# A graph transformer's opening: the second root ahead of the key chain, and two weights' low halves traded between VectorE and GpSimd

## The chip, the cores and the metric

The kernel runs on one core of a Trainium2 chip. The metric is the device time of one execution in microseconds. The engines are TensorE (PE, with its weight loads PEld), VectorE (DVE), ScalarE (ACT), GpSimd (POOL) and SyncE (SP); each has its own instruction queue, executed in order, and they wait for each other through semaphores.

## The reference

Two layers on 1,250 nodes of 512 features, with 21,250 edges. The change lies in the first layer's first step:

```python
xn = _layernorm(x)
x = x + gnn(xn, edge_index, edge_weight, W, b) + mix(xn, w_qkv, w_out, b_out)
# gnn: deg = segment_sum(weights, dst) + 1; norm = dinv[src] * w * dinv[dst]
#      out = segment_sum((xn @ W)[src] * norm, dst) + b
# mix: q, k, v = split(xn @ w_qkv); q = elu(q) + 1; k = elu(k) + 1
#      kv = k^T v per head; out = (q kv) / (q . sum k); out @ w_out + b_out
```

So every normalised node tile is multiplied by four 512x512 weights: key (K), value (V), query (Q) and graph weight (H).

## The kernel before

**Tiles and halves.** The nodes are ten tiles of 128 rows (T = 10). Products keep fp32 accuracy with fp32r operands in two halves: the high half is a rounded copy (`_hi`, ScalarE), the low half is what is left (`_lo`, a subtraction), and a product of a tile with a weight is 4 blocks (one for each 128 of the 512 features) of 3 matmuls (high x high, high x low, low x high). For weight `i` the halves lie in `wsl[:, i, 0]` and `wsl[:, i, 1]`, each in four column blocks `c` of 128x512. For the tiles, TensorE transposes the normalised tile `xn` into the PSUM bank `pT`; `xt_hi(t)` on ScalarE and `xt_lo(t)` on VectorE write the halves of `xT`.

**Normalisation.** For each group of tiles the variance is followed by a root: a power of -0.5 in `root` on GpSimd (line 1015) or a square root on ScalarE, then four Newton steps on VectorE (lines 1311 to 1314) and `nmr` (line 1338), all on 128x5 tiles or smaller. The second root on GpSimd, `root(3, 5, T)`, is for tiles 5 to 9, whose first normalisation comes after pair 5.

**The order of the opening on TensorE**, written out by hand: transposes(0), K0, transposes(1), V0, K1, the edge rows, V1, transposes(2), kv(0), the base row, K2, kv(1), transposes(3), V2, then for t from 3 to 9 K(t), transposes(t+1), V(t), Q(t-3), H(t-3), kv(t). In the first of these rounds `kv(2)` stands behind K3, then a one-column product of `outside` (the count of edges outside their window), then a wait for the flag that VectorE makes of it. A product of tile t waits for `xt_lo(t)`; `kv(t)` = K(t)^T V(t) waits for `k_lo(t)` and `v_lo(t)`, which VectorE makes from the PSUM banks.

**The adjacency matrix.** The sorted edges lie in 170 columns of 128, taken as 85 pairs. Each pair is a product of one-hot matrices: the source one-hots (VectorE, `onehots(g)`, line 1438), times the edge weight's halves (GpSimd, `Loh`, line 1062), against the target one-hots `Roh` within a window (ScalarE for one column, lines 582 and 584, VectorE for the other, line 1440). TensorE places a pair's four matmuls (`adj(g)`, line 2111) between the blocks of the products from the 30th block on: pair 0 after the second block of V3, and the eighth pair, number 7, after the second block of H0. VectorE adds the result into `AT` (line 1469). The target one-hots need `key`, which GpSimd makes in a chain of five operations (lines 1049 to 1053) once VectorE has written `edge` (line 1431). There are four slots for the one-hots of pairs, so VectorE makes those of pairs 0 to 3 ahead.

**Who makes the low halves of the weights.** K and V: VectorE, block by block, in the opening. Q: `split_lo(WQ)` on GpSimd behind the key chain and the second root (line 1007). H: `wh_lo(c)` on VectorE (line 1389), two ahead of `k_elu(2)` and two behind `xt_lo(3)`.

Of the kernel before, what the change touches and what calls it, by code (L numbers as in the profile page):

```python
# [31 lines left out]
T = -(-N // P)  # L32
# [71 lines left out]
def build(nc, a, out):  # L104
    ctx = ExitStack()
    with ctx:
# [240 lines left out]
        for name, first_name, count in (  # L347
# [14 lines left out]
                ("ld_v1", "ld_w3", 16), ("ld_wp", "ld_wo", 16), ("ld_v2", "ld_x", 16), ("ld_xs", "out_st", 0), ("ld_wkb", "ld_small", 0), ("wv_hi", "wk_hi", KC), ("wh_lo", "wv_lo", KC), ("three_var", "c_pool", 1), ("ln_pow0", "pad_zero", 2), ("table_set", "oh_y", 0), ("ld_b2", "b_ld", 32),  # L362
# [137 lines left out]
        def _(act):  # L500
# [96 lines left out]
            split_k(0)  # L597
            ln_sqrt(2, 1, 2)
            split_k(1)
            xt_hi(0)  # L600
# [384 lines left out]
        def _(pool):  # L985
# [18 lines left out]
            def split_lo(i):  # L1004
                pool.wait_ge(S["w_hi"], i - 1)
                for c in range(KC):
                    ins = pool.tensor_tensor(wsl[:, i, 1, c], wraw[:, i, 1, c], wsl[:, i, 0, c].bitcast(F32), ALU.subtract)
                ins.then_inc(S["w_lo"], 1)
# [38 lines left out]
            st(pool.tensor_tensor(whl[:, :, 1], wf, whl[:, :, 0].bitcast(F32), ALU.subtract))  # L1047
            pool.wait_ge(S["edges_ok"], 5)
# [5 lines left out]
            root(3, 5, T)  # L1054
            split_lo(WQ)

            pool.wait_ge(S["keys_ok"], 1)
            for g in range(CP):
                pool.wait_ge(S["oh_src"], g + 1)
                w = whl[:, 2 * g:2 * g + 2, :].bitcast(F32).rearrange("p c (k n) -> p c k n", n=1).broadcast_to([P, 2, 2, P])  # L1060
                o = onehot_[:, g % SLOTS].rearrange("p c (k n) -> p c k n", k=1).broadcast_to([P, 2, 2, P])
                pool.tensor_tensor(Loh[:, g % SLOTS], o, w, ALU.mult).then_inc(S["oh_pool"], 1)  # L1062

# [236 lines left out]
        def _(v):  # L1300
# [86 lines left out]
            def wh_lo(c):  # L1387
                v.wait_ge(S["w_hi"], WH - 1)
                v.tensor_tensor(wsl[:, WH, 1, c], wraw[:, WH, 1, c], wsl[:, WH, 0, c].bitcast(F32), ALU.subtract).then_inc(S["wh_lo"], 1)
# [38 lines left out]
            xt_lo(2)  # L1428
            v2 = lambda x: x.rearrange("p (j c) -> p j c", c=2)
# [4 lines left out]
            ln_roots(3, 5, T, small[:, 2, 5:T])  # L1434
# [8 lines left out]
            def count_outside():  # L1443

                step(v.tensor_scalar(vd, vd, -1.0, 1.0, ALU.mult, ALU.add))
                step(v.tensor_tensor(rest[:, 2, :], wf, vd, ALU.mult))
                step(v.tensor_scalar(vd, rest[:, 2, :], 0.0, None, ALU.not_equal))
                v.tensor_reduce(outside[:], vd, AX, ALU.add).then_inc(S["rest_ok"], 1)
                v.wait_ge(S["rest_ps"], 1)
                v.tensor_copy(flagint[:], pA[0:1, 0:1]).then_inc(S["flag_ok"], 1)  # L1450
# [23 lines left out]
            wh_lo(0)  # L1474
            wh_lo(1)
            k_elu(2)
            xt_lo(3)
            wh_lo(2)
            wh_lo(3)
            k_lo(2)  # L1480
            v_lo(2)
            v.wait_ge(S["keys_ok"], 1)
            count_outside()
            v.wait_ge(S["flag_ok"], 1)
            v.load(count_reg, flagint[0:1, 0:1])
            for g in range(RSLOTS):
                onehots(g)
# [592 lines left out]
        def _(pe):  # L2080
# [34 lines left out]
            def product(t, w, done, bank=None):  # L2115
# [5 lines left out]
                for c in range(KC):  # L2121
                    if t == 0 and w < 2:
                        pe.wait_ge(S[("wk_lo", "wv_lo")[w]], c + 1)
                    if t == 0 and w == WQ:
                        pe.wait_ge(S["w_lo"], 1)
                    if t == 0 and w == WH:
                        pe.wait_ge(S["wh_lo"], c + 1 + after["wh_lo"])
# [608 lines left out]
```

## Time and profile before

| | us |
|---|---|
| Median of three runs | 583.02 (582.8 to 583.6) |
| The profiled execution | 583.02 |
| Its span | 581.3 |
| TensorE busy | 551.8 (95%) |
| VectorE busy | 452.1 (78%) |
| ScalarE busy | 321.4 (55%) |
| GpSimd busy | 278.6 (48%) |

The span runs from the first to the last instruction that the profile shows; 1.7 us of the time lie around it. Busy times of the engines overlap. A row of the timeline gives the start, the busy time, the engine, the line, the operation with output and input, and in brackets how long the engine had been idle and what released it.

### The profile page before, as it was taken

To read this page: it belongs to the slowest core of one execution; us is meant where nothing else is said; L and a number is where in the kernel's file an instruction comes from. 1 tells how busy PE (TensorE), PEld (TensorE's weight loads), DVE (VectorE), ACT (ScalarE), POOL (GpSimd) and SP (SyncE) were. 2 spreads that over 40 slices of the span, in tenths; PEclk is the share of its full clock that TensorE was granted. 3 is DMA by queue.
4 is the path that set the end of the run, shared out by engine and by line. 5 is a ranking of instruction groups with operands and counts; after the bars stand their busy time and mean duration, and the time that the engine had idled before them with its cause. 6 is when DMAs were issued, how large, how long until landed. Compare 5 with 4: busy or idle time off the path is not lost.

```text
span 581.3 us, 8775 instructions
## 1 busy us (share of the span) xinstructions
PE 551.8 (95%) x2947; PEld 451.8 (78%) x2947; DVE 452.1 (78%) x1048; ACT 321.4 (55%) x616; POOL 278.6 (48%) x326
## 2 busy tenths in 40 slices
PE   6968999999999999999999999999999999999997
PEld 4756888888888677888877766778877788778886
DVE  7977899989989688757858878768756765668986
ACT  7856889877855642213134765646455886432252
POOL 4455777777769126434833791002303673031553
PEclk9999999999999999999999999999999999999999
DMA  9500000000002011004104020000002000020004
GB/s 311 173 1 1 1 2 2 2 1 1 2 2 74 24 50 36 23 33 85 33 1 154 2 72 1 0 1 2 0 2 90 1 1 2 2 91 0 1 2 176
DMA packets 15078, 21.12 MB, mean 36 GB/s; under 512 B 3292, under 2 KB 6032, under 8 KB 15034
## 3 DMA queue, kind: packets, MB, share of 16 engines
q1 hardware_dynamic: 13674, 17.94, 9.7%
q10 hardware_dynamic: 1360, 2.62, 1.3%
q8 instruction: 24, 0.39, 0.3%
q14 instruction: 20, 0.16, 0.1%
HBM read 18.00 MB, written 2.56 MB: 35 GB/s over the span
## 4 chain that ended last, share of the span: by engine, by line
PE 60%; DVE 17%; POOL 8%; ACT 6%; issue 5%; DMA 2%; SPq 1%; DVEq 0%; ACTq 0%; POOLq 0%
PE p L2282 7%; PE p L2111 5%; PE pQ L2403 4%; PE p L2403 4%; PE pQ L2129 4%; PE p L2129 4%; PE pH L2129 4%; POOL qx L1236 2%; DVE p L1543 2%; PE p L2369 2%; PE pH L2294 2%; PE pKV L2369 2%; PE pKV L2158 2%; POOL xT L1224 2%; PE pH L2602 1%
## 5 line engine op out<-in xcount | busy, mean ns | idle before, releaser
L1062 POOL TENSOR_TENSOR Loh<-onehot,whl 128x512 fp32r<-128x512 bf16 x85 | 89.4, 1052 | 43.1 <-DVE onehot L1438 43.1
L2282 PE MATMUL p<-G,ATs 128*128 128x512 f32 x300 | 70.5, 391 | 0.0
L2282 PEld LDWEIGHTS p<-G,ATs 128*128 128x128 f32 x300 | 55.9, 188 | 11.6 <-issue 0.2
L2111 PEld LDWEIGHTS p<-Roh,Loh 128*128 128x128 f32 x340 | 49.9, 189 | 13.5 <-issue 6.1
L1438 DVE TENSOR_SCALAR onehot<-iota_src,srclo 128x128 bf16<-128x128 bf16 x170 | 57.5, 379 | 0.7 <-DVE flagint L1450 0.6
L2111 PE MATMUL p<-Roh,Loh 128*128 128x200 f32 x340 | 51.0, 272 | 2.7 <-DVE AT L1469 2.1
L2129 PE MATMUL pQ<-wsl,xT 128*128 128x512 f32 x156 | 44.0, 411 | 7.4 <-DVE xT L1343 7.2
L582 ACT ACTIVATE away<-iota_key,key 128x200 f32<-128x200 f32 x85 | 38.6, 454 | 13.6 <-PE p L2111 13.5
L2129 PE MATMUL pH<-wsl,xT 128*128 128x512 f32 x168 | 45.4, 398 | 0.0
L584 ACT ACTIVATE Roh<-away,onesf 128x200 fp32r<-128x200 f32 x85 | 39.4, 463 | 2.8
L1077 POOL TENSOR_TENSOR ATs<-AT,ATs 128x1280 fp32r<-128x1280 f32 x10 | 30.0, 3002 | 18.6 <-ACT ATs L655 18.3
L2129 PEld LDWEIGHTS pQ<-wsl,xT 128*128 128x128 f32 x156 | 28.0, 197 | 12.9 <-DVE xT L1343 8.0
L1469 DVE TENSOR_TENSOR AT<-AT,p 128x200 f32 x85 | 30.1, 354 | 9.9 <-PE p L2111 9.5
L2129 PE MATMUL p<-wsl,xT 128*128 128x512 f32 x132 | 36.7, 399 | 0.0
L694 ACT ACTIVATE xT<-pT 128x512 fp32r<-128x512 f32 x10 | 6.0, 598 | 54.1 <-PE pT L2269 54.1
L2129 PEld LDWEIGHTS pH<-wsl,xT 128*128 128x128 f32 x168 | 29.2, 189 | 4.3
L1224 POOL TENSOR_TENSOR xT<-xn,xT 128x512 fp32r<-128x512 f32 x10 | 12.9, 1295 | 39.8 <-ACT xT L841 36.9
L2403 PE MATMUL p<-Wk,xT 128*128 128x512 f32 x120 | 30.1, 398 | 0.9 <-ACT rt L802 0.9
L2403 PE MATMUL pQ<-Wq,xT 128*128 128x512 f32 x120 | 29.8, 397 | 0.7 <-DVE xT L1787 0.5
L1215 POOL CAST Wv<-raw 128x512 fp32r<-128x512 f32 x4 | 3.3, 862 | 52.1 <-DVE nmr L1338 52.1
L1440 DVE TENSOR_SCALAR Roh<-iota_key,key 128x200 fp32r<-128x200 f32 x85 | 26.6, 313 | 0.0
L2403 PEld LDWEIGHTS pQ<-Wq,xT 128*128 128x128 f32 x120 | 21.9, 188 | 5.4 <-DVE xT L1787 0.6
(674 smaller groups left out, 1439.2 us busy)
## 6 DMA issues: line engine op xcount, KB each, us to landing
xb<-in_x SPq DMA_DIRECT2D x9, 256.0 KB, 2.6
out<-nodes SPq DMA_DIRECT2D x9, 256.0 KB
raw<-in_L_mix_w_qkv SPq DMA_DIRECT2D x2, 1024.0 KB, 5.1
wraw<-in_L_mix_w_qkv ACTq DMA_DIRECT2D x2, 512.0 KB, 4.9
wraw<-in_L_mix_w_qkv ACTq DMA_DIRECT2D x1, 1024.0 KB, 9.1
nodes<-in_x SPq DMA_DIRECT2D x1, 1024.0 KB, 9.9
wraw<-in_L_mix_w_qkv SPq DMA_DIRECT2D x1, 1024.0 KB, 12.2
wraw<-in_L_gnn_W SPq DMA_DIRECT2D x1, 1024.0 KB, 14.4
```

Source lines behind the costliest of these rows:

```text
L582: act.activation(away[:, g % 2, :], iota_key[:], ACT.Abs, bias=key[:, 2 * g:2 * g + 1], scale=-1.0).then_inc(S["oh_y"], 1)
L584: act.activation(roh(g, 0), away[:, g % 2, :], ACT.Relu, bias=onesf[:, 0:1], scale=-1.0).then_inc(S["oh_act"], 1)
L1062: pool.tensor_tensor(Loh[:, g % SLOTS], o, w, ALU.mult).then_inc(S["oh_pool"], 1)
L1077: pool.tensor_tensor(ATs[:, t % 2, 1], AT[:, :, t * P:(t + 1) * P], ATs[:, t % 2, 0].bitcast(F32), ALU.subtract).then_inc(S["ats_lo"], 1)
L1224: pool.tensor_tensor(xT[:, u, 1].rearrange("p c n -> p (c n)"), xn[:, u, :], xT[:, u, 0].rearrange("p c n -> p (c n)").bitcast(F32), ALU.s ...
L1438: ins = v.tensor_scalar(onehot_[:, g % SLOTS, c, :], iota_src[:], srclo[:, 2 * g + c:2 * g + c + 1], None, ALU.is_equal)
L1440: v.tensor_scalar(roh(g, 1), iota_key[:], key[:, 2 * g + 1:2 * g + 2], None, ALU.is_equal).then_inc(S["oh_dve"], 1)
L1469: v.tensor_tensor(win, win, pW[g % 2][:, 0:T * WIN].rearrange("p (s w) -> p s w", s=T), ALU.add)\
L2111: ins = pe.matmul(pW[g % 2][:, 0:T * WIN], Loh[:, g % SLOTS, c, part, :], roh(g, c), start=(c + part == 0), stop=(c + part == 2))
L2129: ins = pe.matmul(bank[:, :], xT[:, t % XR, x, c, :], wsl[:, w, y, c, :], start=(c == 0 and n == 0), stop=(c == KC - 1 and n == 2))
L2282: ins = pe.matmul(pG[u][:, :], ATs[:, u, x, s_, :], G[:, y, s_, :], start=(s_ + n == 0), stop=(s_ == T - 1 and n == 2))
L2403: ins = pe.matmul(o, xT[:, QT[u], x, c, :], w[:, y, c, :], start=(c + n == 0), stop=(c == KC - 1 and n == 2))
```

## The change

Four things move, all in the first 65 us, and no operation of the arithmetic changes:

- the second `wk_lo` and `xt_lo(0)` change places on VectorE, and on ScalarE `xt_hi(0)` comes ahead of the second `split_k`;
- `root(3, 5, T)` goes ahead of the key chain on GpSimd, and its Newton steps (`ln_roots(3, 5, T)`) ahead of the `edge` subtraction on VectorE;
- the query weight's low halves go from GpSimd to VectorE (three behind `v_lo(1)`, one behind `k_lo(2)`), and the graph weight's from VectorE to GpSimd (two behind the key chain, one each behind the `Loh` of pairs 3 and 4);
- two of the four steps of the count of outside edges go to GpSimd, and VectorE counts and makes the one-hots of pairs 0 and 1 around `v_lo(2)`, before it waits for the flag.

```diff
@@ scalar
             split_k(0)
+            xt_hi(0)
+            split_k(1)
             ln_sqrt(2, 1, 2)
-            split_k(1)
-            xt_hi(0)
             split_k(2)
@@ gpsimd
-            def split_lo(i):
-                pool.wait_ge(S["w_hi"], i - 1)
-                for c in range(KC):
-                    ins = pool.tensor_tensor(wsl[:, i, 1, c], wraw[:, i, 1, c], wsl[:, i, 0, c].bitcast(F32), ALU.subtract)
-                ins.then_inc(S["w_lo"], 1)
+            def wh_lo(c):
+                pool.wait_ge(S["w_hi"], 2)
+                pool.tensor_tensor(wsl[:, WH, 1, c], wraw[:, WH, 1, c], wsl[:, WH, 0, c].bitcast(F32), ALU.subtract).then_inc(S["w_lo"], 1)
...
             st(pool.tensor_tensor(whl[:, :, 1], wf, whl[:, :, 0].bitcast(F32), ALU.subtract))
+            root(3, 5, T)
             pool.wait_ge(S["edges_ok"], 5)
...
             pool.tensor_tensor(key[:], dl, vd, ALU.mult).then_inc(S["keys_ok"], 1)
-            root(3, 5, T)
-            split_lo(WQ)
-
             pool.wait_ge(S["keys_ok"], 1)
+            st(pool.tensor_scalar(vd, vd, -1.0, 1.0, ALU.mult, ALU.add))
+            pool.tensor_tensor(rest[:, 2, :], wf, vd, ALU.mult).then_inc(S["keys_ok"], 1)
+            wh_lo(0)
+            wh_lo(1)
+
             for g in range(CP):
...
                 pool.tensor_tensor(Loh[:, g % SLOTS], o, w, ALU.mult).then_inc(S["oh_pool"], 1)
+                if g in (3, 4):
+                    wh_lo(g - 1)
@@ vector
-            def wh_lo(c):
-                v.wait_ge(S["w_hi"], WH - 1)
-                v.tensor_tensor(wsl[:, WH, 1, c], wraw[:, WH, 1, c], wsl[:, WH, 0, c].bitcast(F32), ALU.subtract).then_inc(S["wh_lo"], 1)
+            def wq_lo(c):
+                v.wait_ge(S["w_hi"], 1)
+                v.tensor_tensor(wsl[:, WQ, 1, c], wraw[:, WQ, 1, c], wsl[:, WQ, 0, c].bitcast(F32), ALU.subtract).then_inc(S["wq_lo"], 1)
...
             wk_lo(0)
+            xt_lo(0)
             wk_lo(1)
-            xt_lo(0)
...
             xt_lo(2)
+            ln_roots(3, 5, T, small[:, 2, 5:T])
             v2 = lambda x: x.rearrange("p (j c) -> p j c", c=2)
             v.wait_ge(S["e_pe"], 2)
             v.tensor_tensor(v2(dl), v2(rest[:, 0, :]), ..., ALU.subtract).then_inc(S["edges_ok"], 1)
             k_lo(1)
             v_lo(1)
-            ln_roots(3, 5, T, small[:, 2, 5:T])
+            for c in range(3):
+                wq_lo(c)
...
             def count_outside():
-                step(v.tensor_scalar(vd, vd, -1.0, 1.0, ALU.mult, ALU.add))
-                step(v.tensor_tensor(rest[:, 2, :], wf, vd, ALU.mult))
+                v.wait_ge(S["keys_ok"], 2)
                 step(v.tensor_scalar(vd, rest[:, 2, :], 0.0, None, ALU.not_equal))
                 v.tensor_reduce(outside[:], vd, AX, ALU.add).then_inc(S["rest_ok"], 1)
+
+            def outside_counted():
                 v.wait_ge(S["rest_ps"], 1)
                 v.tensor_copy(flagint[:], pA[0:1, 0:1]).then_inc(S["flag_ok"], 1)
...
-            wh_lo(0)
-            wh_lo(1)
             k_elu(2)
             xt_lo(3)
-            wh_lo(2)
-            wh_lo(3)
             k_lo(2)
+            wq_lo(3)
+            count_outside()
+            onehots(0)
             v_lo(2)
-            v.wait_ge(S["keys_ok"], 1)
-            count_outside()
+            onehots(1)
+            outside_counted()
             v.wait_ge(S["flag_ok"], 1)
             v.load(count_reg, flagint[0:1, 0:1])
-            for g in range(RSLOTS):
+            for g in range(2, RSLOTS):
                 onehots(g)
@@ tensor, product(t, w, done)
                     if t == 0 and w == WQ:
-                        pe.wait_ge(S["w_lo"], 1)
+                        pe.wait_ge(S["wq_lo"], c + 1 + after["wq_lo"])
                     if t == 0 and w == WH:
-                        pe.wait_ge(S["wh_lo"], c + 1 + after["wh_lo"])
+                        pe.wait_ge(S["w_lo"], c + 1)
```

## Rows read from the trace of the kernel before

**Rows 1.** Windows, core 0: from:to, length, busy of each engine, granted clock, DMA.
```profile
35.40:40.80 5.40, 0.03 (x2) 0.00 (x1) 5.26 (x9) 0.61 (x2) 2.59 (x3) 0.99 0.00 0
40.80:43.00 2.20, 2.20 (x5) 1.81 (x6) 2.20 (x4) 2.17 (x5) 0.00 (x0) 0.50 0.01 4
...
47.00:62.00 15.00, 12.81 (x69) 9.86 (x70) 14.42 (x42) 10.73 (x23) 10.37 (x10) 1.00 0.01 2
62.00:170.00 108.00, 107.52 (x663) 93.85 (x662) 99.24 (x327) 89.28 (x196) 78.54 (x76) 1.00 0.00 1
```

**Rows 2.** Timeline at K3: start us, busy us, engine, line, operation, [idle before].
```profile
26.96 0.69 DVE L1343 TENSOR_TENSOR xT<-pT,xT 128x512 fp32r<-128x512 f32 x1 [0.30 <-ACT xT L537]
...
28.00 0.33 DVE L1431 TENSOR_TENSOR edge<-rest,p 128x170 f32<-128x170 f32 x1 [0.35 <-PE p L2179]
...
28.49 0.80 POOL L1049 TENSOR_SCALAR edge<-edge 128x170 f32<-128x170 f32 x1 [2.45 <-DVE edge L1431]
...
28.92 0.68 DVE L1356 TENSOR_TENSOR vhl<-pQ,vhl 128x512 fp32r<-128x512 f32 x1
...
29.38 0.56 POOL L1050 TENSOR_TENSOR edge<-edge 128x170 f32<-128x170 f32 x1
...
31.85 1.19 POOL L1015 TENSOR_TENSOR rstd<-small,lomask 128x5 f32<-128x5 f32 x1
...
32.45 2.98 PE L2129 MATMUL p<-wsl,xT 128*128 128x512 f32 x12
...
33.02 4.97 POOL L1007 TENSOR_TENSOR wsl<-wraw,wsl 128x512 fp32r<-128x512 f32 x4
...
33.08 1.25 DVE L1311 TENSOR_TENSOR small<-rstd 128x5 f32<-128x5 f32 x1 [3.48 <-POOL rstd L1015]
...
38.25 1.29 DVE L1389 TENSOR_TENSOR wsl<-wraw,wsl 128x512 fp32r<-128x512 f32 x2
...
40.80 4.54 PE L2129 MATMUL pQ<-wsl,xT 128*128 128x512 f32 x12 [5.37 <-DVE xT L1343]
```

**Rows 3.** Timeline of the start.
```profile
6.36 0.16 DVE L1311 TENSOR_TENSOR small<-rstd 128x1 f32<-128x1 f32 x1
...
7.13 0.16 DVE L1338 SCALAR_TENSOR_TENSOR nmr<-mv,rstd 128x1 f32<-128x1 f32 x1
...
10.23 0.69 DVE L1381 TENSOR_TENSOR wsl<-wraw,wsl 128x512 fp32r<-128x512 f32 x1 [0.19 <-ACT wsl L520]
...
18.32 0.41 POOL L1032 TENSOR_SCALAR frow<-frow 128x256 f32<-128x256 f32 x1
```

**Rows 4.** Timeline at 224 and 233 us, one line of VectorE twice.
```profile
224.66 1.83 DVE L1622 SCALAR_TENSOR_TENSOR nodes<-nodes,dinv,xb 128x512 f32<-128x512 f32 x1
...
233.34 0.74 DVE L1622 SCALAR_TENSOR_TENSOR nodes<-nodes,dinv,xb 128x512 f32<-128x512 f32 x1
```

**Rows 5.** Timeline from the third value tile to the flag.
```profile
42.46 0.68 DVE L1356 TENSOR_TENSOR vhl<-p,vhl 128x512 fp32r<-128x512 f32 x1
...
43.71 0.25 DVE L1447 TENSOR_SCALAR edge<-rest 128x170 f32<-128x170 f32 x1
...
45.18 1.45 PE L2158 MATMUL pKV<-vhl,khl 128*128 128x130 f32 x12
...
46.78 0.15 DVE L1450 CAST flagint<-p 1x1 int32<-1x1 f32 x1 [2.46 <-PE p L2190]
```

**Rows 6.** Timeline of the first pairs.
```profile
47.58 0.42 DVE L1438 TENSOR_SCALAR onehot<-iota_src,srclo 128x128 bf16<-128x128 bf16 x2 [0.65 <-DVE flagint L1450]
...
47.91 0.32 DVE L1440 TENSOR_SCALAR Roh<-iota_key,key 128x200 fp32r<-128x200 f32 x1
...
52.01 0.31 DVE L1440 TENSOR_SCALAR Roh<-iota_key,key 128x200 fp32r<-128x200 f32 x1
...
60.33 0.35 DVE L1469 TENSOR_TENSOR AT<-AT,p 128x200 f32 x1
...
60.82 0.67 PE L2111 MATMUL p<-Roh,Loh 128*128 128x200 f32 x4
```

More of the change, by code:

```diff
@@ L361, in build @@
                 ("y2_ok", "y_ok", T), ("ld_q1", "ld_w0", 16), ("ld_k1", "ld_w1", 16), ("ld_u1", "ld_w2", 16),
-                ("ld_v1", "ld_w3", 16), ("ld_wp", "ld_wo", 16), ("ld_v2", "ld_x", 16), ("ld_xs", "out_st", 0), ("ld_wkb", "ld_small", 0), ("wv_hi", "wk_hi", KC), ("wh_lo", "wv_lo", KC), ("three_var", "c_pool", 1), ("ln_pow0", "pad_zero", 2), ("table_set", "oh_y", 0), ("ld_b2", "b_ld", 32),
+                ("ld_v1", "ld_w3", 16), ("ld_wp", "ld_wo", 16), ("ld_v2", "ld_x", 16), ("ld_xs", "out_st", 0), ("ld_wkb", "ld_small", 0), ("wv_hi", "wk_hi", KC), ("wq_lo", "wv_lo", KC), ("three_var", "c_pool", 1), ("ln_pow0", "pad_zero", 2), ("table_set", "oh_y", 0), ("ld_b2", "b_ld", 32),
                 ("ld_f1", "ld_edge", 16 * 9), ("x9_ok", "at_done", 1), ("first_ok", "x9_ok", 1), ("c2_ok", "x2_ok", 2), ("ln_pow", "pads_ok", 4), ("o6_ps", "ft_ps", 3), ("o6_ok", "kvd_ok", 6)):
```

## The prediction

> **What bounds the kernel now.** I first read the busy time of the engines by stage [rows 1]. From 62 to 170 us TensorE is busy for 107.52 of 108.00 us. There is nothing to win there but a move of the whole stage, and from this stage on every microsecond by which TensorE starts earlier is one off the end. In two stretches before it TensorE isn't the bound. From 35.40 to 40.80 it does 0.03 us of work, with VectorE busy for 5.26. From 47 to 62 it idles 2.19 of 15 us, with VectorE busy for 14.42.
>
> Then I read the timeline around the first stretch [rows 2]. The fourth key product, K3 (the `pQ` row) starts at 40.80 after 5.37 us of idle time, released by VectorE's `xt_lo(3)`, line 1343. VectorE itself had waited 3.48 us, until 33.08, for GpSimd's second root (line 1015, 31.85 to 33.04), which stood behind the key chain (lines 1049 to 1053). Its four Newton steps then took from 33.08 to about 38.0, some 1.2 us each. The same steps on small tiles took 0.16 each, five of them 0.93 us in all (6.36 to 7.29) [rows 3]. GpSimd was in the four 128x512 subtractions of line 1007 meanwhile, 1.24 us each. So each step waited for one of them.
>
> The granted clock was 0.50 of full speed from 40.80 to 43.00 [rows 1], the 1.2 GHz level, right after the idle stretch. The 12 products of K3 took 4.54 us where the 12 before took 2.98 [rows 2]. So the stall costs 5.37 + 1.56 = 6.93 us.
>
> **The change, part by part. Start of the opening.** VectorE idled 0.19 us before its second `wk_lo` [rows 3]. With `xt_lo(0)` in that place the gap closes, and VectorE's queue is what the next 15 us follow. I take 0.15 (ends 0 and 0.19).
>
> **Root ahead of the chain, Newton steps ahead of the `edge` subtraction.** The root needs GpSimd for 1.19 us from about 26.1, until 27.3. There it stands in a gap: GpSimd idled 2.45 us before line 1049 [rows 2]. `xt_lo(2)` ends at 27.65, 0.15 earlier now: 27.50. The Newton steps have GpSimd quiet beside them, since the key chain waits for line 1431 behind them: 0.95 us, to 28.45. Line 1431 takes 0.33, to 28.78, where it ended at 28.33. So the key chain starts 0.45 later, at 28.94. Behind line 1431 VectorE does `k_lo(1)` and `v_lo(1)`, to 30.07, still before K2 ends (35.43 - 0.15 less V2, 2.98, less `kv(1)` and transposes), so no product waits for them.
>
> **Query weight's low halves on VectorE.** Four subtractions of 0.65 (1.29 for two) replace the same four for the graph weight, so VectorE's own work is unchanged. Their place is new: beside the key chain. There two rows decide. A VectorE operation with both inputs in SBUF took 1.83 us when a GpSimd operation on a 128x512 tile started at the same instant and 0.74 otherwise [rows 4]. `v_lo`, whose one input is in PSUM, took 0.68 with GpSimd busy (28.92) and 0.68 with it idle (42.46) [rows 2, 5]. So I let `wq_lo` and each GpSimd operation take turns, and leave the PSUM readers free. Line 1050 ends at 28.94 + 0.89 + 0.56 = 30.39. Three `wq_lo` (1.95) and the three steps left of the chain (31.88 - 29.94, less three gaps of 0.08: 1.70) then alternate. VectorE is out at 30.39 + 1.95 + 1.15 = 33.49, and the key is made at 34.04, where it was made at 31.88. SyncE, which waits for the key too, has nothing to load before the pairs are done, and nobody but ScalarE needs the key at once, and in its queue `v_hi(2)`, which waits for V2, stands ahead of the first use.
>
> The Trainium skill, SBUF — State Buffer, section "Who interferes with whom", states this as a rule against the change: a VectorE instruction with two SBUF inputs and a GpSimd one that reads SBUF exclude each other for the whole instruction. The two durations above agree. By the rule the sum is the one worked out here; without it, that of the first rival.
>
> **K3.** From 33.49 VectorE does `k_elu(2)` and `xt_lo(3)`, 0.65 each: 34.8. V2 ends at 35.28. So K3 waits for nothing, with 0.5 us to spare, and at the full clock it ends at 35.28 + 2.98 = 38.26, against 45.34.
>
> **What is late next: `v_lo(2)`.** In the new order it is queued behind `k_lo(2)`, `wq_lo(3)`, the count with its wait for the second `keys_ok`, and `onehots(0)`; `kv(2)`, the flag, the transposes and V3 on TensorE wait for it. `k_lo(2)` ends at 35.4. GpSimd has taken over two steps of the count: a two-step scalar operation, between 0.41 for 256 columns [rows 3] and 0.80 (line 1049), of which I take 0.4, being the same kind, and a product of 0.55; with gaps, to 35.15. Its `wh_lo(0)`, 1.25, runs until 36.45, and `wq_lo(3)` waits for it: 37.1. `wh_lo(1)` runs to 38.35 and holds up the scalar operation of the count. Count (43.71 to 44.32, 0.61): 39.0. `onehots(0)` (47.58 to 48.23, 0.65): 39.65. `v_lo(2)`: 40.25. TensorE waits 2 us for it. From the start of `kv(2)` to the flag the profile has 46.93 - 45.18 = 1.75 [rows 5], so the flag stands at about 42.05, against 46.93: 4.88 earlier.
>
> **From the flag to the eighth pair.** That pair's products start at 60.82, released by the accumulation that ends at 60.68 on VectorE [rows 6]: 13.89 after the flag. VectorE made the one-hots of pairs 0 to 3 in this stretch, 47.58 to 52.32. Two are now made before the flag: -2.7. `wh_lo(2)` and `wh_lo(3)` now stand in GpSimd's queue behind pairs 3 and 4, in front of the following products, and the one-hot writes of VectorE give way to them: up to 2 x 1.25, of which I take 2.4, as the two 1.2 us waits of the Newton steps. Net about -0.25. H0 needs the last of these halves. The one-hots come at a pitch of (52.01 - 47.91) / 3 = 1.37, so `wh_lo(3)` is done at about 42.7 + 3 x 1.37 + 2 x 1.25 = 49.3, and H0, eight blocks of three products (8 x 2.98 / 4 = 6.0) and six pairs behind the flag, comes after 50. TensorE's own work in the stretch, 13.9 less the 2.2 of idle time [rows 1], is 11.7 and doesn't bind.
>
> Sum: -4.88 - 0.25 = -5.1 us. The profiled execution took 583.02 us, 581.3 of them its span, and is the median itself. So 577.9.
>
> **The rivals.** *The waits on both sides are less dear* (25%). If `wq_lo` slips between GpSimd's operations, or `wh_lo` between VectorE's, `v_lo(2)` is done before K3 ends; the flag comes at 38.26 + 1.75 = 40.0, -6.9. For it: Newton's 0.16 us steps cost GpSimd nothing. Against it: the 1.83 us row. Time: 583.02 - 7.0 = 576.0; with the halves between the pairs free as well the stretch after the flag shrinks to TensorE's 11.7 and the gain is 9.1, which I give little.
>
> *The pair stage pays more* (18%). The pitch of 1.37 us a pair is near what GpSimd's product needs, and two extra subtractions put it 2 x 1.25 us behind, which may come on top of what VectorE loses; or TensorE's idle time before `v_lo(2)` brings the 1.2 GHz level again, 1.56 us by K3's example. Against the latter: TensorE idled 2.19 us between 47 and 62, in pieces, at a granted clock of 1.00 [rows 1]. One of these on top of the sum gives -3.3: 579.7.
>
> *The gain is lost on the way* (8%). If the early start only lengthens waits in the VectorE-bound stretch from 47 to 62, nothing over 1 us arrives: 582.5. Against it: no row there waits for anything but VectorE's own queue, which starts with the flag.
>
> *Slower, by `v_lo(2)` behind the key* (4%). Each microsecond by which the second `keys_ok` and `wh_lo(1)` come later is one for `kv(2)`. It would take 5.1 us more than my 38.35, thus `v_lo(2)` after 45.3. If VectorE's PSUM readers too had to wait for GpSimd's operations, six of them stand between 28.8 and `v_lo(2)`'s end, at up to 1.25 each: four such waits give 5.0, about the old time, and six 7.5, which is 585.4. It decides against the change from the fifth on. Against it: `v_lo` at 28.92, in 0.68 beside GpSimd.
>
> **How the numbers follow.** The forecast, -4.2 to -6.2, has 45%. The range goes from the cheap rival to the dear one: 575.4 to 580.0, that is 7.6 to 3.0 us off. No change and change can be told apart by 0.2%, 1.2 us. Faster by more than that: 45 + 25 + 18 = 88%; within it 8%; slower 4%.
>
> **What would show it.** In the changed profile: K3 starts within 0.3 us of V2's end, and no clock of 0.50 about 41 us. The Newton steps at line 1311 and after are 0.16 to 0.2 us each. `wq_lo` shows about 1.2 us for some of its four, and GpSimd's steps show lengths above those of before. `kv(2)` waits 1 to 2.5 us for `v_lo(2)`. The flag is at 41.5 to 42.5, and the eighth pair 5 us earlier. I am wrong if TensorE waits at V3 or K3 for the bank or for the root, if the idle time before `kv(2)` is over 3 us, or if the clock falls again.

## The result, and the profile after

The changed kernel takes 574.79 us (median of 4 runs, 574.37 to 575.44), the kernel before 583.07 beside it: a ratio of 0.9849, with a 95% interval of 0.9820 to 0.9878. That is 8.3 us faster. Forecast were 5.1 us, 577.9, with a range from 575.4 to 580.0: the sign was right, the gain too small, and the time came out 0.6 us below the range.

The profiled execution has a span of 573.7 us, 7.6 less. These are the rows of its opening that answer to [rows 2, 3, 5]; lines have moved by up to six in the code (VectorE's Newton steps from 1311 to 1314, `wq_lo` is line 1392, `wh_lo` line 1006).

```profile
8.27 0.69 DVE L1371 BATCH_NORM_STATS2 stat<-nodes 128x6 f32<-128x512 f32 x1 [0.98 <-DMA nodes<-in_x]
...
25.88 1.20 POOL L1013 TENSOR_TENSOR rstd<-small,lomask 128x5 f32<-128x5 f32 x1 [0.17 <-DVE small L1329]
...
27.25 0.15 DVE L1314 TENSOR_TENSOR small<-rstd 128x5 f32<-128x5 f32 x1
...
28.04 0.17 DVE L1341 SCALAR_TENSOR_TENSOR nmr<-mv,rstd 128x5 f32<-128x5 f32 x1
28.24 0.33 DVE L1435 TENSOR_TENSOR edge<-rest,p 128x170 f32<-128x170 f32 x1
...
28.66 0.81 POOL L1048 TENSOR_SCALAR edge<-edge 128x170 f32<-128x170 f32 x1 [1.58 <-DVE edge L1435]
...
29.69 2.60 DVE L1392 TENSOR_TENSOR wsl<-wraw,wsl 128x512 fp32r<-128x512 f32 x3
30.20 0.98 POOL L1050 TENSOR_SCALAR edge<-edge 128x170 f32<-128x170 f32 x1
...
31.26 0.48 POOL L1051 TENSOR_TENSOR edge<-edge,rest 128x170 f32<-128x170 f32 x1
...
31.82 0.89 POOL L1052 TENSOR_TENSOR key<-edge 128x170 f32<-128x170 f32 x1
...
33.05 0.69 DVE L1346 TENSOR_TENSOR xT<-pT,xT 128x512 fp32r<-128x512 f32 x1
...
33.68 2.99 POOL L1006 TENSOR_TENSOR wsl<-wraw,wsl 128x512 fp32r<-128x512 f32 x2
34.25 1.27 DVE L1392 TENSOR_TENSOR wsl<-wraw,wsl 128x512 fp32r<-128x512 f32 x1
...
34.95 2.88 PE L2134 MATMUL pQ<-wsl,xT 128*128 128x512 f32 x12
...
35.45 1.34 DVE L1451 TENSOR_SCALAR edge<-rest 128x170 f32<-128x170 f32 x1
...
37.62 0.68 DVE L1359 TENSOR_TENSOR vhl<-p,vhl 128x512 fp32r<-128x512 f32 x1
...
38.45 1.53 PE L2163 MATMUL pKV<-vhl,khl 128*128 128x130 f32 x12 [0.62 <-DVE vhl L1359]
...
40.14 0.14 DVE L1456 CAST flagint<-p 1x1 int32<-1x1 f32 x1 [1.09 <-PE p L2195]
```

The five steps of the Newton group now take 0.96 us (27.25 to 28.21), where four took 5. K3 starts without a wait and takes 2.88 us. Then comes the wait that the prediction named: `kv(2)` for `v_lo(2)`, but with 0.62 us, not 2.

The pair stage, which answers to [rows 6]:

```profile
42.95 0.36 DVE L1475 TENSOR_TENSOR AT<-AT,p 128x200 f32 x1
...
43.23 1.91 DVE L1443 TENSOR_SCALAR onehot<-iota_src,srclo 128x128 bf16<-128x128 bf16 x2
...
43.79 1.29 POOL L1006 TENSOR_TENSOR wsl<-wraw,wsl 128x512 fp32r<-128x512 f32 x1
...
46.23 1.27 POOL L1006 TENSOR_TENSOR wsl<-wraw,wsl 128x512 fp32r<-128x512 f32 x1
...
46.98 0.67 PE L2116 MATMUL p<-Roh,Loh 128*128 128x200 f32 x4 [1.16 <-DVE AT L1475]
...
52.59 0.35 DVE L1475 TENSOR_TENSOR AT<-AT,p 128x200 f32 x1
...
53.08 0.67 PE L2116 MATMUL p<-Roh,Loh 128*128 128x200 f32 x4 [0.26 <-DVE AT L1475]
```

The eighth pair stands at 53.08, against 60.82. The one-hots of the fifth pair (43.23) are held up to 1.91 us by the subtraction on GpSimd at 43.79. The 15 us from the flag on, which [rows 1] show from 47 to 62, are here those from 40.35 to 55.35. In them TensorE idles 1.55 us, where it idled 2.19, and VectorE is busy for 14.40 us, where it was busy for 14.42. So VectorE still bounds this stage. The stage behind is as full as before, with TensorE busy for 107.47 of 108 us:

```profile
40.35:55.35 15.00, 13.45 (x76) 10.95 (x77) 14.40 (x39) 11.45 (x25) 11.57 (x11) 1.00 0.01 1
53.00:161.00 108.00, 107.47 (x661) 93.93 (x662) 99.23 (x328) 89.24 (x197) 78.63 (x75) 1.00 0.01 1
```

**How the experiments are read.** Run times of one kernel scatter by one to five us, landmarks within a run by much less. What moves the start is when the second tile lands; VectorE's statistics of it begin at 8.27 here and at 8.35 before:

```profile
8.35 0.69 DVE L1368 BATCH_NORM_STATS2 stat<-nodes 128x6 f32<-128x512 f32 x1 [1.06 <-DMA nodes<-in_x]
```

So I take four landmarks in each profile and subtract the start of that row: the start of K3 (its length in brackets), the end of the flag, the start of the eighth pair, and the start of the long reduction over `AT` on VectorE (11.9 us), which comes when all pairs are in.

| kernel | K3 | flag | pair 8 | reduction | median, its ratio to before |
|---|---|---|---|---|---|
| before | 32.45 (4.54) | 38.58 | 52.47 | 166.19 | |
| changed | 26.68 (2.88) | 32.01 | 44.81 | 158.49 | 574.79, 0.9849 |
| changed, again | 26.67 (2.88) | 32.01 | 44.81 | 158.47 | 574.63, 0.9856 |
| root alone | 26.91 (2.88) | 32.17 | 46.06 | 159.80 | 575.81, 0.9858 |
| root back | 31.00 (4.61) | 37.18 | 49.97 | 163.62 | 580.04, 0.9931 |
| start alone | 32.16 (4.87) | 38.63 | 52.53 | 166.28 | 583.95, 0.9991 |
| start undone | 26.95 (2.88) | 32.27 | 45.07 | 158.74 | 575.02, 0.9857 |
| one-hots late | 26.70 (2.88) | 31.17 | 48.53 | 162.08 | 576.97, 0.9873 |
| `v_lo` first | 26.64 (2.88) | 31.42 | 44.20 | 157.88 | 574.52, 0.9835 |
| halves ahead | 26.86 (2.88) | 33.91 | 46.09 | 159.75 | 576.14, 0.9871 |
| halves zeroed | 26.64 (2.88) | 31.97 | 43.34 | 156.98 | 573.50, 0.9826 |
| behind pairs 0, 1 | 26.79 (2.88) | 32.59 | 44.81 | 158.49 | 574.71, 0.9842 |
| in the gap | 26.65 (2.88) | 31.48 | 43.70 | 157.33 | 573.78, 0.9833 |
| in the gap, again | 26.66 (2.88) | 31.50 | 43.72 | 157.37 | 573.82, 0.9834 |
| 18 products | 34.53 (3.12) | 39.25 | 53.14 | 166.89 | 582.21, 0.9967 |
| 11 products | 33.30 (3.02) | 37.91 | 51.81 | 165.54 | 580.46, 0.9938 |

From the eighth pair to the reduction every kernel takes 113.5 to 113.8 us. What is won by the eighth pair is kept: 7.66 us of the change, 7.70 at the reduction.

Two kernels were profiled twice, and their landmarks repeat to 0.04 us. The others have one profile each, the kernel before among them. Its profile was taken in a run at a mean granted clock of 0.996. Beside the experiments it ran 62 times more, on four chips: the nine runs at 0.996 or above took 581.3 to 583.3 us, and the fourteen at 0.988 or below took 584.6 to 587.0. The ten runs of the changed kernel are all at 0.999 or 1.000. So some of what its medians win beyond the landmarks may be low clock that the median run of the kernel before still has; the runs without a trace can't show where. One more run of the kernel before was slow, at 1,899 us, and is left out of the ratios.

### The profile page after: what moved, and what is told of

Read it like the earlier page. It is cut to its first block, busy times and chain, and to the rows that moved or that the text cites. A ratio compares the mean times of both kernels' runs of the same rounds, so it can differ in the third digit from the quotient of the medians.

```text
span 573.7 us, 8774 instructions
## 1 busy us (share of the span) xinstructions
PE 550.4 (96%) x2947; PEld 450.9 (79%) x2947; DVE 449.6 (78%) x1046; ACT 321.2 (56%) x616; POOL 280.8 (49%) x328
## 4 chain that ended last, share of the span: by engine, by line
PE 63%; DVE 16%; POOL 8%; issue 6%; ACT 4%; DMA 2%; SPq 1%; DVEq 0%; ACTq 0%; POOLq 0%
PE p L2287 7%; PE p L2116 6%; PE pH L2134 5%; PE pQ L2408 5%; PE p L2134 4%; PE p L2408 4%; PE pQ L2134 4%; POOL qx L1239 2%; DVE p L1548 2%; PE pKV L2163 2%; PE p L2374 2%; PE pH L2299 2%; PE pKV L2374 2%; POOL xT L1227 2%; PE pQ L2607 1%
## 5 line engine op out<-in xcount | busy, mean ns | idle before, releaser
L2134 PE MATMUL pQ<-wsl,xT 128*128 128x512 f32 x156 | 42.4, 399 | 1.7 <-DVE xT L1346 0.8
```

The source lines that it names most:

```text
L2134: ins = pe.matmul(bank[:, :], xT[:, t % XR, x, c, :], wsl[:, w, y, c, :], start=(c == 0 and n == 0), stop=(c == KC - 1 and n == 2))
```

## The experiments

**Root alone.** The kernel before with the root and its Newton steps moved, nothing else.

```diff
@@ gpsimd
+            root(3, 5, T)
             pool.wait_ge(S["edges_ok"], 5)
...
             pool.tensor_tensor(key[:], dl, vd, ALU.mult).then_inc(S["keys_ok"], 1)
-            root(3, 5, T)
@@ vector
             xt_lo(2)
+            ln_roots(3, 5, T, small[:, 2, 5:T])
...
             v_lo(1)
-            ln_roots(3, 5, T, small[:, 2, 5:T])
```

> The kernel before with one part of the change alone: the second root ahead of the key chain on GpSimd, its Newton steps ahead of the edge subtraction on VectorE. The halves of both weights, the count and the one-hots stay as they were. Theory A (the root's place is the gain, and instructions of VectorE and GpSimd cost each other only part of their length): K3 starts with the end of V2 at about 35.4, the flag comes at 40.3 to 40.6, the four one-hots behind it take as long as before, total 6.3 to 6.8 us faster. Theory B (whole instructions exclude each other, as the prediction priced it): the four subtractions on VectorE meet the four of the query weight on GpSimd, the flag comes at 42 or later, total at most 5 us faster. Theory C (most of the gain lies in the one-hots and halves that were moved): at most 4 us.

Measured: 575.81 us, a ratio of 0.9858 (0.9815 to 0.9901); flag 6.41 us earlier, eighth pair 6.41 earlier. Theory A. The other edits add 0.16 us at the flag to this and 1.25 at the eighth pair. The trade of the halves isn't what makes this possible: here VectorE's four subtractions for the graph weight stand beside GpSimd's four for the query weight, and both stretch, without K3 waiting.

```profile
31.21 1.96 DVE L1389 TENSOR_TENSOR wsl<-wraw,wsl 128x512 fp32r<-128x512 f32 x2 [1.21 <-ACT wsl L516]
...
32.58 6.58 POOL L1007 TENSOR_TENSOR wsl<-wraw,wsl 128x512 fp32r<-128x512 f32 x4
...
34.29 2.38 DVE L1389 TENSOR_TENSOR wsl<-wraw,wsl 128x512 fp32r<-128x512 f32 x2
...
35.17 2.88 PE L2129 MATMUL pQ<-wsl,xT 128*128 128x512 f32 x12
...
40.28 0.15 DVE L1450 CAST flagint<-p 1x1 int32<-1x1 f32 x1 [0.28 <-PE p L2190]
```

GpSimd's four take 6.58 us instead of 4.97 [rows 2], VectorE's pairs 1.96 and 2.38 instead of 1.29.

**Root back.** The changed kernel with the root behind the chain and the Newton steps behind `v_lo(1)`.

```diff
@@ gpsimd
-            root(3, 5, T)
             pool.wait_ge(S["edges_ok"], 5)
...
             pool.tensor_tensor(key[:], dl, vd, ALU.mult).then_inc(S["keys_ok"], 1)
+            root(3, 5, T)
@@ vector
             xt_lo(2)
-            ln_roots(3, 5, T, small[:, 2, 5:T])
...
             v_lo(1)
+            ln_roots(3, 5, T, small[:, 2, 5:T])
             for c in range(3):
                 wq_lo(c)
```

> The changed kernel with the second root behind the key chain again, and its Newton steps behind v_lo(1) on VectorE; all else as changed. Theory A: VectorE waits for the root until about 33, the three query halves, k_elu(2) and xt_lo(3) follow, K3 starts at 37.5 to 39.5 and the clock falls again or not according to the wait; total 1.5 to 4 us faster than the kernel before. Theory C: what was moved besides the root carries the gain, total over 5 us faster.

Measured: 580.04 us, 0.9931 (0.9905 to 0.9958). K3 is 4.3 us later than in the changed kernel and takes 4.61 us, at the low clock. All the other edits together, without the root, bring 2.50 us at the eighth pair. Theory A again.

**Start alone, and start undone.** The first exchange by itself on the kernel before, and taken out of the changed kernel.

```diff
@@ scalar
             split_k(0)
-            ln_sqrt(2, 1, 2)
+            xt_hi(0)
             split_k(1)
-            xt_hi(0)
+            ln_sqrt(2, 1, 2)
@@ vector
             wk_lo(0)
+            xt_lo(0)
             wk_lo(1)
-            xt_lo(0)
```

> The kernel before with the first exchange alone (xt_lo(0) ahead of the second wk_lo, xt_hi(0) ahead of the second split_k). Theory A: VectorE's operations follow each other at 0.60 instead of 0.87 there, everything up to 28 us comes 0.27 earlier; but K3 is 5.4 us late by the root, which moves with the edge rows, so 0.2 to 0.35 us at the end. Rival: the 0.35 us seen in the changed kernel was an earlier landing of the second tile, and this gives nothing.

> The changed kernel without the exchange at its start (xt_lo(0) and xt_hi(0) back behind the second weight blocks). Theory A (alone on the kernel before, the exchange brought K3 0.29 us forward and a longer stretch at the low clock took it back; here no low clock stands behind it): all landmarks, measured from the landing of the second tile, come 0.25 to 0.3 us later than in the changed kernel. Rival: the exchange is absorbed by the edge rows or ScalarE here too, under 0.1 us.

Measured: alone 583.95 us, 0.9991 (0.9970 to 1.0013), no change. K3 starts 0.29 us earlier and takes 0.33 longer, 4.87, as it runs longer at a granted clock of 0.50. In this profile the clock was at 0.50 from 38.5 us on, within the idle stretch, and still at 45.0. Windows of this run on the core, the columns as in [rows 1], the granted clock third from the end:

```profile
38.50:41.30 2.80, 0.00 (x0) 0.00 (x0) 2.73 (x7) 0.59 (x2) 0.02 (x1) 0.50 0.00 0
41.32:43.00 1.68, 1.68 (x4) 1.39 (x5) 1.68 (x4) 1.65 (x4) 0.00 (x0) 0.50 0.02 5
...
44.00:45.00 1.00, 1.00 (x4) 0.76 (x3) 0.77 (x3) 0.97 (x3) 0.00 (x0) 0.50 0.00 0
```

In the kernel before the clock was still full up to 40.6 us, and at 0.50 from 40.8 to 44.0:

```profile
38.50:40.60 2.10, 0.00 (x0) 0.00 (x0) 2.10 (x4) 0.41 (x1) 0.00 (x0) 1.00 0.00 0
40.80:44.00 3.20, 3.20 (x8) 2.52 (x9) 3.10 (x8) 3.13 (x7) 0.00 (x0) 0.50 0.01 3
```

Whether the exchange made the low stretch longer isn't shown by one profile of each kernel. The runs of this kernel lie at mean clocks of 0.990 to 0.996 and those of the kernel before at 0.987 to 0.997, so the low stretches of the kernel before differ in length by themselves.

Undone in the changed kernel, where no low clock follows, all landmarks come 0.25 to 0.27 us later. So the exchange is worth 0.26 us where it can arrive. The medians, 575.02 beside 574.63, don't tell this apart.

**The clock alone: 18 and 11 products.** Products on a constant keep TensorE at work ahead of K3 in the kernel before.

```diff
@@ tensor
             for t in range(LAG, T):
+                if t == LAG:
+                    pe.wait_ge(S["v_lo"], 2)
+                    keep_busy(18, pQ)     # 11 in the second run
                 k_product(t)
```

> The kernel before, with 18 products on a constant in the idle stretch ahead of K3 (into K3's own bank, overwritten by it). It prices the clock alone. Theory A: K3 runs at the full clock in 3.0 us instead of 4.5, the flag follows from it, and all of it reaches the end: 1.3 to 1.6 us faster. Rival: VectorE's one-hots are the bound behind it, and nothing arrives (within 0.3 us).

> The kernel before with 11 products on a constant instead of 18 in the idle stretch ahead of K3: at 0.44 us each they end before xt_lo(3), so that K3 isn't late. Theory A: K3 takes 3.0 us, the flag and the eighth pair come 1.5 us earlier (from the landing of the second tile), total 1.3 to 1.7 us faster. Rival: the clock has fallen by the end of the last 0.5 us or VectorE is the bound behind K3, nothing arrives.

Measured: 18 took 7.9 us, so that K3 was late by them (a misjudged length: 0.44 us each); 11 ended in time, but in that profile the opening itself was 0.9 us late by `xt_hi(2)`. Its granted clock had been at 0.50 early in it, as this run's window shows:

```profile
12.50:15.80 3.30, 3.30 (x9) 2.56 (x8) 3.23 (x8) 3.28 (x6) 0.00 (x0) 0.50 1.06 359
```

From K3's start to the eighth pair the kernel before takes 20.02 us, these two 18.61 and 18.51. So the low clock behind the stall costs the profiled kernel before 1.4 to 1.5 us, and that arrives at the eighth pair. The medians, 582.21 and 580.46, are 1.7 and 3.6 us below the kernel before (by the first ratio 1.9). By the landmarks the first kernel is 0.7 us later than the kernel before at the eighth pair, and the second 0.7 earlier. The medians thus say more than the landmarks explain; the fastest runs of the second and of the kernel before on its chip, 579.73 and 581.26, differ by 1.5. The 21 runs of the two kernels lie at mean granted clocks of 0.997 to 1.000, those of the kernel before beside them at 0.987 to 0.997, and its times rise as that clock falls. That is the likely reason, but with one trace for each kernel it stays open.

**Side by side.** The disputed cost by itself: behind the last result VectorE subtracts 128x512 tiles six times while GpSimd does the same on 170 or 512 columns. It was run once.

```python
for i in range(6):   # VectorE, x in SBUF or in PSUM
    v.tensor_tensor(qbuf[:, 4 + i, 0:D], x[:, 0:D], nodes[:, 2, 0:D], ALU.subtract)
for i in range(n):   # GpSimd, w = 170 or 512
    pool.tensor_tensor(AT[:, i, 0:w], nodes[:, 3, 0:w], nodes[:, 4, 0:w], ALU.subtract)
```

> The changed kernel with a measurement behind its last result, which makes it some 30 us longer: VectorE subtracts alone (six of 128x512, both inputs in SBUF), GpSimd alone (four of 512 columns, four of 170), then both at once: VectorE's six beside eight of 170 columns, beside four of 512, and six with one input in PSUM beside four of 512. Theory B (whole instructions exclude each other): 6 x 0.65 + 8 x 0.55 = 8.3 us and 6 x 0.65 + 4 x 1.25 = 8.9 us for the two pairs of queues. Theory A (only the part that moves data does, with some 0.2 us of GpSimd's and 0.1 of VectorE's free): 5.5 to 6.8 and 7.5 to 8.2. With one input in PSUM neither waits: 5.0.

In this run's timeline the first row is VectorE alone; then beside eight GpSimd operations of 170 columns (581.50), beside four of 512 (588.38), and with one input in PSUM beside four of 512 (596.45):

```profile
570.57 3.70 DVE L2101 TENSOR_TENSOR qbuf<-nodes 128x512 f32<-128x512 f32 x6
...
581.50 5.44 DVE L2101 TENSOR_TENSOR qbuf<-nodes 128x512 f32<-128x512 f32 x6 [7.23 <-POOL AT L1304]
588.38 7.96 DVE L2101 TENSOR_TENSOR qbuf<-nodes 128x512 f32<-128x512 f32 x6 [1.44 <-POOL AT L1304]
596.42 4.94 POOL L1304 TENSOR_TENSOR AT<-nodes 128x512 f32<-128x512 f32 x4 [1.23 <-DVE qbuf L2101]
596.45 3.68 DVE L2101 TENSOR_TENSOR qbuf<-p,nodes 128x512 f32<-128x512 f32 x6
```

And this run's windows of the two middle phases, GpSimd's busy time being the fifth:

```profile
581.40:588.30 6.90, 0.00 (x0) 0.00 (x0) 5.44 (x6) 0.00 (x0) 6.76 (x9) 0.50 0.00 0
588.30:596.40 8.10, 0.00 (x0) 0.00 (x0) 7.96 (x6) 0.00 (x0) 6.75 (x5) 0.50 0.00 0
```

With one input in PSUM neither queue waits: 3.68 us, and 4.94 for GpSimd's four, which took 4.92 alone. With both inputs in SBUF the two queues alternate, and the first of VectorE's six, which starts ahead of GpSimd, takes 0.69 us as alone. Five then meet a GpSimd operation of 170 columns (0.54 us alone), and each is (5.44 - 3.70) / 5 = 0.35 us longer. Four meet one of 512 columns (1.26 alone), and each is (7.96 - 3.70) / 4 = 1.07 longer.

Alone, VectorE's operations follow each other at 0.60 us, and GpSimd's at 0.50 and 1.22. One of each takes 0.95 us with the short ones and 1.67 with the long, where the sums are 1.10 and 1.82. So whole instructions nearly exclude each other, and 0.15 us of each such round is free at either length. The first phase takes 6.84 us until GpSimd's last operation ends, at the upper end of theory A (6.8) and not theory B's 8.3.

**One-hots late.** `v_lo(2)` ahead of the count, and all four one-hots behind the flag, as before the change.

```diff
             k_lo(2)
             wq_lo(3)
-            count_outside()
-            onehots(0)
             v_lo(2)
-            onehots(1)
+            count_outside()
             outside_counted()
...
-            for g in range(2, RSLOTS):
+            for g in range(RSLOTS):
```

> The changed kernel with v_lo(2) ahead of the count, and the one-hots of pairs 0 and 1 behind the flag again. Theory A: v_lo(2) is done before K3 ends, so the flag comes 0.6 us earlier (39.6), but two more one-hots of 1.35 us each stand behind it: 1.5 to 2.2 us slower than the changed kernel. Rival: the one-hots are hidden behind V3 anyway, and it is as fast or 0.6 us faster.

Measured: 576.97 us, 0.9873 (0.9842 to 0.9904). In the profile the flag is 0.84 us earlier than in the changed kernel, the eighth pair 3.72 later, twice what theory A had. The fourth pair waits 2.24 us, in this run's timeline:

```profile
48.43 1.15 PE L2114 MATMUL p<-Roh,Loh 128*128 128x200 f32 x4 [2.24 <-DVE AT L1475]
```

And the clock falls in the middle of the pair stage, as this run's windows ahead of that row and behind it show:

```profile
46.20:48.40 2.20, 0.00 (x0) 0.00 (x1) 2.20 (x6) 0.94 (x2) 2.07 (x3) 0.76 0.00 0
48.40:54.00 5.60, 5.57 (x17) 4.83 (x18) 4.64 (x17) 3.39 (x8) 3.81 (x5) 0.50 0.00 0
```

The profiled run was the slowest of the four, 578.13 us. The two at mean granted clocks of 0.999 and 1.000 took 575.83 and 576.52, which is 1.0 and 1.7 us above the changed kernel's median. So without a fall of the clock the order of the one-hots seems to cost near what theory A had (1.5 to 2.2), and the rest of the 3.72 goes with the clock, which doesn't fall in every run.

**`v_lo` first.** Only `v_lo(2)` is taken ahead of `onehots(0)`.

```diff
             count_outside()
-            onehots(0)
             v_lo(2)
+            onehots(0)
             onehots(1)
```

> The changed kernel with v_lo(2) directly behind the count and ahead of onehots(0). Theory A: TensorE's wait of 0.62 us ahead of kv(2) goes, the one-hots of pairs 0 and 1 are still done at the flag, 0.5 to 0.6 us faster than the changed kernel. Rival: the pair stage is bound by VectorE's work and takes it back, within 0.2 us.

Measured: 574.52 us, 0.9835 (0.9808 to 0.9861). Flag 0.59 and eighth pair 0.61 us earlier than in the changed kernel: theory A. The medians, 574.52 and 574.79, don't tell the two apart.

**Halves ahead.** All four graph halves on GpSimd ahead of the pairs, none between them.

```diff
-            wh_lo(0)
-            wh_lo(1)
+            for c in range(KC):
+                wh_lo(c)
...
-                if g in (3, 4):
-                    wh_lo(g - 1)
```

> The changed kernel with all four subtractions of the graph weight on GpSimd ahead of the pairs, none between them. Theory A (two between the pairs hold up VectorE's one-hots by 1.0 and 0.6 us, and pair 3's products 1.2 us): GpSimd's first product comes 2 us later but still before it is needed at 42.2, the pair stage is shorter, 1 to 1.6 us faster. Rival (theory B): they hold up the count and the one-hots ahead of v_lo(2) instead, by up to 2.5 us, and it is 1 us slower or more.

Measured: 576.14 us, 0.9871 (0.9843 to 0.9899); the flag 1.90 and the eighth pair 1.28 us later than in the changed kernel. The rival was right, by this row: `onehots(0)`, with its one-input scalar operations, waits for GpSimd's queue too (2.14 us instead of 0.41), and `v_lo(2)` stands behind it.

```profile
33.37 5.47 POOL L1006 TENSOR_TENSOR wsl<-wraw,wsl 128x512 fp32r<-128x512 f32 x4
...
36.75 2.14 DVE L1441 TENSOR_SCALAR onehot<-iota_src,srclo 128x128 bf16<-128x128 bf16 x2
...
39.87 1.53 PE L2161 MATMUL pKV<-vhl,khl 128*128 128x130 f32 x12 [2.35 <-DVE vhl L1357]
```

Behind that wait of 2.35 us the granted clock was at 0.50 here too, as this run's window shows, so a part of the 1.28 us is the clock's:

```profile
41.50:44.80 3.30, 3.06 (x10) 2.57 (x10) 2.14 (x7) 1.41 (x3) 1.66 (x2) 0.50 0.00 0
```

**Halves zeroed.** The two subtractions between the pairs are left out, and zeros written.

```diff
                 if g in (3, 4):
-                    wh_lo(g - 1)
+                    pool.memset(wsl[:, WH, 1, g - 1].bitcast(F32), 0.0).then_inc(S["w_lo"], 1)
```

> The changed kernel without the two subtractions between the pairs: the third and fourth low halves of the graph weight are set to zero instead, a write of 0.5 us that reads nothing, so part of the graph product is left out. Theory A: the two subtractions cost VectorE's one-hots 1.0 and 0.6 us, so the eighth pair comes 1.0 to 1.6 us earlier than in the changed kernel, from the landing of the second tile. Rival (they are hidden as TensorE is the bound there): under 0.3 us.

Measured: 573.50 us, 0.9826 (0.9786 to 0.9866); from the flag to the eighth pair 11.37 us instead of 12.80. So the two subtractions cost 1.43 us there, theory A's range. That is what they cost beyond the two writes in their place, which took 0.57 and 0.53 us on GpSimd.

**In the gap, and behind pairs 0 and 1.** Both take `v_lo(2)` ahead of `onehots(0)`. The first has the third half ahead of the pairs and the fourth behind pair 1, the second has them behind pairs 0 and 1. GpSimd's edit of the first:

```diff
-            wh_lo(0)
-            wh_lo(1)
+            for c in range(3):
+                wh_lo(c)
...
-                if g in (3, 4):
-                    wh_lo(g - 1)
+                if g == 1:
+                    wh_lo(3)
```

> The changed kernel with v_lo(2) ahead of onehots(0), the third graph half on GpSimd ahead of the pairs and the fourth behind pair 1, in the time in which GpSimd waits for the flag. Theory A (what stands between pairs 3 and 5 costs VectorE 1.0 and 0.6 us, what stands in the gap costs nothing): measured from the landing of the second tile, the flag comes 0.6 us earlier than in the changed kernel and the eighth pair 1.5 to 2.2 us earlier. Rival: the third half delays onehots(0) and (1) as in the run with all halves ahead, and the pairs begin later; the eighth pair is within 0.5 us of the changed kernel's.

> The changed kernel with v_lo(2) ahead of onehots(0), the last two graph halves on GpSimd behind pairs 0 and 1. Theory A: GpSimd's gap before the flag takes both but for 0.5 us; VectorE's onehots(1) is held up by about 1 us, before the flag, where nobody waits for it; the eighth pair 1.5 to 2.2 us earlier than in the changed kernel, as measured from the landing of the second tile. Rival: the two push the products of pairs 1 and 2 back by 2.5 us and TensorE waits for them, no gain.

> The changed kernel itself, on the same chip as the two beside it. Theory A: its landmarks repeat within 0.1 us, its time differs from run to run by the landing of the second tile (7.8 to 9.2 us) and by which of VectorE and GpSimd takes an operation on xb first at about 216 us, which is worth 1 to 1.5 us. Rival: the landmarks themselves move, and the differences between the kernels of half a microsecond are noise.

> The kernel with v_lo(2) ahead of onehots(0), the third graph half ahead of the pairs and the fourth behind pair 1, a second time, beside the changed kernel. Theory A: its eighth pair stands 1.1 us ahead of the changed kernel's as in the first run, and its median is 0.6 to 1.6 us lower. Rival: the medians can't be told apart or lie the other way, as the share of runs that lose 1.2 us at 216 us outweighs it.

Measured: in the gap 573.78 us, 0.9833 (0.9802 to 0.9864), the eighth pair 1.11 us ahead of the changed kernel's; again 573.82, 0.9834 (0.9807 to 0.9860), 1.09 ahead, beside the changed kernel's 574.63 on the same chip. By landmarks this version beats the change by 1.1 us; the medians say 0.8, within their scatter. That is less than the 1.5 to 2.2 expected. The fourth half didn't fall into the gap before the flag (39.82): GpSimd came to it at 40.61, and VectorE's one-hots of the third pair took 1.49 us beside it, where they took 0.42 in the kernel before [rows 6]. The first run's timeline:

```profile
40.47 1.49 DVE L1443 TENSOR_SCALAR onehot<-iota_src,srclo 128x128 bf16<-128x128 bf16 x2 [0.66 <-DVE flagint L1456]
...
40.61 1.29 POOL L1006 TENSOR_TENSOR wsl<-wraw,wsl 128x512 fp32r<-128x512 f32 x1
```

The fourth pair still waits 1.15 us for VectorE. Behind pairs 0 and 1 (574.71 us, 0.9842, 0.9812 to 0.9872) gains nothing: `onehots(1)` takes 2.26 us, and VectorE, held by it, makes the flag 1.1 us later than in the other.

## Why the forecast was too small

1. *K3's stall and its cause*: right. The root alone, its place on both engines, brings 6.41 of the 7.66 us at the eighth pair. The root cost nothing in GpSimd's gap, as argued.
2. *The low clock, 1.56 us*: right in size (1.4 to 1.5 by the added products), for the execution that was profiled.
3. *Start, 0.15 of an idle gap of 0.19*: too small, 0.26. VectorE's operations of this length follow each other at 0.60 us, and an idle gap in the trace starts when the operation ends, at 0.68; the room lost was 10.23 - 9.36 - 0.60 = 0.27.
4. *"Three `wq_lo` (1.95) and the three steps left of the chain then alternate. VectorE is out at ... 33.49"*: this is the step that failed. VectorE was out at 32.29, and the key was made at 32.71, not 34.04. The sum made each of VectorE's three wait for one of GpSimd's to end, which put 33.49 - 30.07 - 1.95 = 1.47 us of waiting on VectorE. Measured was 0.72: the three took 2.60 us, and three in a row take 0.60 + 0.60 + 0.68 = 1.88 alone. Of the 1.20 us by which VectorE was early, this is 0.75; the rest is `v_lo(1)`, which ended at 29.77 and not 30.07, and the 0.65 taken for 0.60. The key chain, priced at 5.10 us (28.94 to 34.04), took 4.05 (28.66 to 32.71).

   The rows that the step rested on, 1.83 against 0.74 [rows 4], are of a 1.29 us operation beside VectorE's. The same whole turns were charged for operations of 0.5 us. Side by side a short one costs 0.35, not 0.54; three of those would be 1.05. Here the meetings were fewer too: GpSimd's operation at 31.26 took 0.48, as in the kernel before (0.49). The long meetings behind it were priced about right: the two `wh_lo` took 2.99 us for 3.2 (35.15 to 38.35), and `wq_lo(3)` 1.27. So `v_lo(2)` ended at 38.30, not 40.25, and 1.33 of these 1.95 us are the earlier key. The wait ahead of `kv(2)` was 0.62, not 2. Flag: 6.57 earlier by landmarks, not 4.88. The first rival (25%) came close to that, with 6.9, by waits that are less dear; but its condition, `v_lo(2)` done before K3 ends, wasn't met (38.30 against 37.83).
5. *The pair stage, -2.7 + 2.4*: the one-hots' term was about right (2.5 with the halves zeroed, 13.89 - 11.37), the halves' too dear: 1.43 for 2.4. Measured net -1.09, and -2.7 + 1.43 = -1.27. The danger named beside it, that TensorE's idle time in this stage brings the low clock back, didn't come true in the changed kernel.

So 1.7 us of the missing 2.6 at the eighth pair come from steps 3 and 4, and 0.8 from step 5. In steps 4 and 5 whole durations of one engine were charged to the other; step 3 was a misread gap. The last 0.6 us up to the medians' 8.3 are within their interval (7.1 to 10.5).

The condition that the prediction put on a loss, that VectorE's PSUM readers wait for GpSimd, is ruled out by the side-by-side phase with PSUM (3.68 us for six, 3.70 alone). The clock as a danger in the pair stage was real: with the one-hots late (a wait of 2.24 us) and with the halves ahead (2.35) it fell. In the changed kernel the longest wait there was 1.16 us, and the granted clock stayed at 1.00.

## What to carry to other kernels

When a short operation's result is wanted by one engine and made by another behind a chain that can't start yet, look in the second engine's queue for the gap before the chain: the move is free there and was worth 6.4 us here. Where VectorE and GpSimd hold each other up, don't carry the price of a long meeting over to short ones: measure one of each kind (0.35 and 1.07 us for the same VectorE operation here), and sort the operations that read PSUM out first. And count landmarks from a common event inside the run: in two kernels profiled twice they repeated to 0.04 us, where medians of six runs could not order two kernels 0.3 us apart. But look at the granted clock of the run too: a landmark behind a low stretch belongs to that execution.

## What the hardware showed unexpectedly

**A coin toss at 216 to 225 us.** [Rows 4] show VectorE at 1.83 us and 0.74. This isn't a fixed property of the kernel: it goes by whether GpSimd, which the landing of `xb` releases, starts ahead of VectorE. In the first profile of the changed kernel GpSimd was 0.1 us ahead; in its second VectorE took 0.74. With `v_lo` first VectorE was ahead too, and GpSimd waited instead, 1.75 us for 1.3. The timeline of the changed kernel:

```profile
216.90 1.74 DVE L1627 SCALAR_TENSOR_TENSOR nodes<-nodes,dinv,xb 128x512 f32<-128x512 f32 x1
```

The timeline of `v_lo` first:

```profile
216.54 0.74 DVE L1627 SCALAR_TENSOR_TENSOR nodes<-nodes,dinv,xb 128x512 f32<-128x512 f32 x1
```

When VectorE loses, TensorE waits for it before its next transposes, as in the timeline of the kernel before:

```profile
231.40 0.66 PE L2269 MATMUL pT<-ident,xn 128*128 128x128 f32 x4 [1.19 <-DVE xn L1570]
```

In the profiles from the reduction to the end of the span there are 405.3 to 405.9 us for most kernels whose VectorE won, and 406.2 to 407.0 for most that lost; the two runs with products on a constant lost and have 405.1 and 405.3, so this isn't all of the tail's scatter. It may be a good part of why run times differ by a microsecond while the landmarks stand; that the runs without a trace do the same isn't shown.

**A small gain that didn't arrive.** With the start exchange alone, K3 began 0.29 us earlier, stood longer at the 1.2 GHz level, and ended 0.04 later. That starting earlier caused the longer stretch isn't shown. What is shown is that the same exchange brings 0.26 us at every landmark of the changed kernel, where no low stretch follows it.

**What a meeting costs.** The Trainium skill, SBUF — State Buffer, section "Who interferes with whom", says that a VectorE instruction with at most one SBUF input doesn't contend with GpSimd outside the 2-port perf modes. The same page of the Trainium skill, section "Summary: rules for kernel authors", says that with two SBUF inputs, against a GpSimd operation that reads SBUF, the second to issue "fully blocks" until the first finishes. The first agrees for subtractions with one input in PSUM (3.68 and 4.94 us side by side, 3.70 and 4.92 alone). The one-hots, scalar operations with one input in SBUF, did wait (2.14 us instead of 0.41); in which mode they ran no run here shows. On the second the measurement decides: 0.35 us was lost to an operation of 0.54, and 1.07 to one of 1.26, so it holds but for about 0.2 us of each GpSimd operation.
